# Slot norms moved from the slot matrix to the logits, and combine logits spread between the first expert steps of a soft mixture

## Chip, cores and metric

The kernel runs on one core of one Trainium2 chip. It is one launch that holds a whole twelve-part network (four levels, each of cross attention, attention and feed-forward). The metric is the device time of one execution in microseconds (us).

## The reference, cut to what matters

The change touches two parts of level 1: a linear attention with decay, and after it a soft mixture of 16 experts with 128 slots each, on 2 batches of 128 tokens with 256 features.

```python
# level 1 attention (16 heads of width 16)
q = phi(x @ w_q); k = phi(x @ w_k); v = x @ w_v          # phi(z) = elu(z) + 1
running_kv   = decay_scan(k * v)                          # s_t = decay * s_{t-1} + x_t
running_ksum = decay_scan(k)
den = clip(sum_over_head(q * running_ksum), 1e-6)
x = x + (q * running_kv / den) @ w_out

# level 1 feed-forward: soft mixture, E = 16 experts, S = 128 slots
x_ln = layernorm(x) * gamma + beta
x_n  = x_ln / |x_ln| * scale
mu_n = mu / |mu|                                          # |.| over the 256 features: one number per slot
logits   = einsum('bnd,des->bnes', x_n, mu_n)
dispatch = softmax over tokens n;  combine = softmax over all 2048 slots
slot_in  = einsum('bnd,bnes->besd', x_ln, dispatch)
h        = gelu(slot_in @ W1[e] + b1[e]);  slot_out = h @ W2[e] + b2[e]
x = x + einsum('bsd,bns->bnd', slot_out, combine)
```

## The kernel before, in words

TensorE (PE) multiplies, VectorE (DVE) and ScalarE (ACT) evacuate PSUM and do the elementwise work, GpSimd (POOL) has little to do, SyncE (SP) issues the DMAs. Each of the five runs its own list in order, written out by hand, and they meet at semaphores (`wait_ge`, `then_inc`); `link` makes VectorE wait for its own instruction. Each part of the network is one block, and all engines meet at its end. `k.bank(i)` is one of the eight PSUM banks of 512 float32 columns.

**The slot norms.** The norms of the 2048 slots are found on the way to level 1: `k.mu_norm` holds 1/|mu| in four groups of 32 equal rows, group j for slots 512j to 512j+511 (`l1_xattn`, L1044 and L1084 to L1085).

**`l1_attn`** (L1096 to L1207). PE turns x, makes k, q and v (24 matmul passes with `a_w_qkv`), then with a selecting matrix (`quadrant_rows`) spreads the four groups of `mu_norm` over all partitions in banks 5, 6, 7, 4 (L1139). ACT copies each bank to `row`, which is half of the tensor `mu_squares` (L1162), and POOL multiplies both feature halves of the slot matrix `mu` by it in place, in eight instructions (L1172 to L1177). `mu_ready` counts to 4. Meanwhile DVE makes k and q from the banks (L1187), kv (L1190), and runs the decayed sums as eight scans of 128 elements: four of k into `a_run_k` and four of kv into `a_run_kv` (L1196). It multiplies both by q (L1199, L1200); PE sums over heads (L1142); DVE clips, inverts and multiplies (L1202 to L1204); PE multiplies by `w_out` (L210, from a helper that all accumulating products share); DVE adds to x (L1207).

**`l1_ffn`** (L1214 to L1455). SP issues the loads of b1, W1 (two halves) and W2, all counted by `w_loaded[5]`, and then one small load of b2 for each expert. DVE makes `f_x_ln` and the unit-length `f_x_l`; PE turns the latter (L1263), ACT copies it to `f_x_l_T` (L1349). Then PE computes all combine logits, 128 tokens by 2048 slots for each batch, in eight pieces of 512 columns that fill all eight banks (`combine_logits`); DVE takes the maximum of each piece (L1398), and ACT exponentiates a whole batch at once out of four banks into `comb` (L1352). After that come the experts, as a software pipeline: in step i PE does `dispatch_logits(i)` (4 passes of 256 columns, bank 0), `turn(i-1)` (transposes of two `comb` blocks and of two `disp` blocks, all in bank 1), `gather(i-2)`, `hidden(i-3)`, `slot_out(i-4)` and `combine(i-5)`; the steps run from 0 to 20.

```python
steps = (dispatch_logits, turn, gather, hidden, slot_out, combine)
for i in range(ne + len(steps) - 1):
    for lag, step in enumerate(steps):
        if 0 <= i - lag < ne:
            step(i - lag)
```

`dispatch_logits(i)` may begin once ACT has exponentiated those of i-1 out of the same bank. In step i DVE does `dispatch_max(i)` (L1406, L1408), `take_turned(i-1)` (two copies, `f_disp_tok` and `f_combT`, L1421 and L1424), `take_slots(i-2)` (L1430), `add_bias(i-4)` (L1438) and `dispatch_norm(i)` (L1413, L1415), which waits for ACT's exponentials and lets PE turn them in the next step. ACT does the exponentials of step i (two ACTIVATEs, L1361) and the Gelu of i-3 (L1369). From step 3 on it loads a table before each of the two.

Of the kernel before, what the change touches and what calls it, by code (L numbers as in the profile page):

```python
# [17 lines left out]
P = 128  # L18
# [1077 lines left out]
def l1_attn(k):  # L1096
# [3 lines left out]
    with ExitStack() as ctx:  # L1100
# [8 lines left out]
        row = k.musq[:, 1]  # L1109
# [3 lines left out]
        with signals(nc, k.pool, "dve_step xt_ready proj_ready low_ready exp_ready dec_ready scanned den_in_psum den_ready o_ready out_ready "  # L1113
                     "select_ready row_in_psum row_taken") as s, nc.Block() as block:
# [12 lines left out]
            def _(pe):  # L1127
# [24 lines left out]
            def _(act):  # L1152
# [7 lines left out]
                for j in range(4):  # L1160
                    act.wait_ge(s.row_in_psum, j + 1)
                    nc.scalar.copy(row[:, j * 512:(j + 1) * 512], k.bank(ROW_BANK[j])).then_inc(s.row_taken, 1)  # L1162

            @block.gpsimd
            def _(pool):
# [5 lines left out]
                for j in range(4):  # L1171
                    pool.wait_ge(s.row_taken, j + 1)  # L1172
                    for c in range(DC):
                        sl = slice(j * 512, (j + 1) * 512)
                        last = nc.gpsimd.tensor_tensor(k.mu[:, c, sl], k.mu[:, c, sl], row[:, sl], ALU.mult)
                    last.then_inc(k.mu_ready, 1)

            @block.vector
            def _(dve):
# [5 lines left out]
                for j, bank, dst in ((0, 1, kk), (1, 0, q)):  # L1185
                    dve.wait_ge(s.exp_ready, j + 1)
                    link(nc.vector.scalar_tensor_tensor(out=flat(dst), in0=k.bank(bank), scalar=0.0, in1=ex[:, j],  # L1187
                                                        op0=ALU.max, op1=ALU.add))
                dve.wait_ge(s.proj_ready, 3)
# [24 lines left out]
def l1_ffn(k):  # L1214
# [5 lines left out]
    CR = 6  # L1220
    with ExitStack() as ctx:
        def sb(name, shape, dt=F32):
# [11 lines left out]
        ct = sb("combT", [P, CR, BT])  # L1234
# [6 lines left out]
                 "logits_ready cmax_ready cexp_ready dlog_ready dmax_ready dexp_ready disp_ready "  # L1241
                 "t_in_psum t_taken slot_in_psum slot_taken h_in_psum h_taken so_in_psum so_taken b2_loaded0 b2_loaded1 out_added")
        with signals(nc, k.pool, names) as s, nc.Block() as block:
# [14 lines left out]
            def _(pe):  # L1258

                def turn_x(b):  # L1260
                    pe.wait_ge(s.xs_ready, b + 1)
                    for c in range(DC):
                        last = nc.tensor.transpose(k.bank(7 - b, P, T, c * T), xs[:, b, c * P:(c + 1) * P], k.ident[:])  # L1263
                    last.then_inc(s.xT_in_psum, 1)

                def combine_logits(b, j):
                    pe.wait_ge(s.xT_ready, b + 1)
                    pe.wait_ge(k.mu_ready, j + 1)
                    if b and j >= 2:
                        pe.wait_ge(s.xT_ready, B)  # L1270
                    matmul_acc(nc, k.bank(4 * b + j), [(xst[:, c, b * T:(b + 1) * T], k.mu[:, c, j * 512:(j + 1) * 512]) for c in range(DC)]
                               ).then_inc(s.logits_ready, 1)
                turn_x(0)
                combine_logits(0, 0)
                turn_x(1)
                for j in range(1, 4):
                    combine_logits(0, j)
                for j in range(4):
                    combine_logits(1, j)
                pe.wait_ge(s.cexp_ready, 1)  # L1280

                def dispatch_logits(e):
                    if e >= 1:
# [3 lines left out]
                def turn(e):  # L1287

                    pe.wait_ge(s.cexp_ready, B)
                    if e >= 1:  # L1290
                        pe.wait_ge(s.t_taken, e)
                    for b in range(B):
                        nc.tensor.transpose(k.bank(1, P, P, BT + b * T), comb[:, b, e * SLOTS:(e + 1) * SLOTS], k.ident[:])
# [3 lines left out]
                    last.then_inc(s.t_in_psum, 1)  # L1297

# [27 lines left out]
                def combine(e):  # L1326
                    pe.wait_ge(s.so_taken, B * (e + 1))
                    for b in range(B):
                        last = nc.tensor.matmul(k.bank(5 + b, P, D), ct[:, e % CR, b * T:(b + 1) * T], so[:, e % 2, b],
                                                start=(e == 0), stop=(e == ne - 1))  # L1330
                    last.then_inc(s.out_added, 1)
                steps = (dispatch_logits, turn, gather, hidden, slot_out, combine)
                for i in range(ne + len(steps) - 1):
                    for lag, step in enumerate(steps):
                        if 0 <= i - lag < ne:
                            step(i - lag)

            @block.scalar
            def _(act):
# [7 lines left out]
                for b in range(B):  # L1347
                    act.wait_ge(s.xT_in_psum, b + 1)
                    nc.scalar.copy(xst[:, :, b * T:(b + 1) * T], k.bank(7 - b, P, DC * T).rearrange("p (c t) -> p c t", c=DC)).then_inc(s.xT_ready, 1)  # L1349
                for b in range(B):  # L1350
                    act.wait_ge(s.cmax_ready, b + 1)
                    nc.scalar.activation(comb[:, b], k.ps[:, 4 * b:4 * b + 4].rearrange("p a n -> p (a n)"), ACT.Exp, bias=sm[:, b, 4:5],  # L1352
                                         accum_out=sm[:, b, 5:6]).then_inc(s.cexp_ready, 1)
                act.wait_ge(k.w_loaded[5], 64)
                for i in range(ne + 3):
                    if i < ne:
                        act.wait_ge(s.dmax_ready, B * (i + 1))
# [14 lines left out]
            def _(dve):  # L1372
# [22 lines left out]
                for b in range(B):  # L1395
                    for j in range(4):
                        dve.wait_ge(s.logits_ready, 4 * b + j + 1)
                        last = nc.vector.reduce_max(mx4[:, b, j:j + 1], k.bank(4 * b + j), AX.X)  # L1398
                    link(last)
                    link(nc.vector.reduce_max(sm[:, b, 10:11], mx4[:, b], AX.X))  # L1400
# [1648 lines left out]
```

## Time and profile before

| | |
|---|---|
| median of 3 runs | 1909.32 us (1905.56, 1909.32, 1909.6) |
| the profiled execution | 1906.26 us, its span 1904.5 us |
| PE busy / DVE / ACT / POOL, share of the span | 83% / 61% / 47% / 25% |
| mean granted TensorE clock | 0.911 of full speed |
| `l1_attn` in the trace | 514.4 to about 550.3 us |
| `l1_ffn` in the trace | 550.4 to about 667.6 us |

An engine is busy while an instruction of it runs; a PE that is busy may run at half clock, which the granted clock tells (1.00 is 2.4 GHz, 0.50 is 1.2 GHz). A float32 product appears as two passes, so that a product of 256 features is four matmul records. Averages over the span say nothing on these two blocks, which make up 8% of it, so that everything that follows is read from their own stretch of the trace.

### The profile page before, as it was taken

How to read it: one execution, taken by the hardware profiler on the slowest of the kernel's cores; microseconds unless marked ns; L12 is line 12 of the kernel's file. 1: busy time of each engine (PE TensorE's matmuls, PEld its weight loads, DVE VectorE, ACT ScalarE, POOL GpSimd, SP SyncE). 2: the span in 40 equal slices, each digit the busy share in tenths (PEclk: the TensorE clock that was granted, in tenths of full speed). 3: DMA queues.
4: the chain of work that ended last, by engine and by line, in shares of the span. 5: the costliest groups of instructions: out<-in, count | busy, mean ns of one | idle time of the engine just before them, and what ended most of it. 6: DMA issues, size and time to landing. Idle time of an engine off the chain costs nothing. (4 is left out here: it accounts for less than half of the span.)

```text
span 1904.5 us, 25717 instructions
## 1 busy us (share of the span) xinstructions
PE 1575.8 (83%) x8888; PEld 1102.6 (58%) x8888; DVE 1159.7 (61%) x2417; ACT 886.0 (47%) x1979; POOL 484.8 (25%) x490
## 2 busy tenths in 40 slices
PE   7969888499859988655899999999976578888778
PEld 5644444377536744544577778877752245555567
DVE  5779997366566534545446653455338778888843
ACT  1559988211326532222334533433333478888821
POOL 2350000000020000003322431243000088888810
PEclk9978999699979999657899999999989889999969
DMA  3008999354020000112000000000021322223010
GB/s 122 1 1 161 183 186 178 127 168 146 28 50 14 26 28 1 34 31 98 1 1 1 1 1 1 1 1 1 1 73 55 99 85 82 85 82 100 1 41 32
DMA packets 189501, 110.90 MB, mean 58 GB/s; under 512 B 149129, under 2 KB 165514, under 8 KB 188477
## 3 DMA queue, kind: packets, MB, share of 16 engines
q1 hardware_dynamic: 189372, 109.26, 22.1%
q8 instruction: 73, 1.20, 0.3%
q14 instruction: 56, 0.45, 0.1%
HBM read 75.41 MB, written 0.26 MB: 40 GB/s over the span
## 5 line engine op out<-in xcount | busy, mean ns | idle before, releaser
L210 PE MATMUL banks<-a_w_ring,x_normed_T 128*128 128x512 f32 x320 | 151.1, 613 | 13.2 <-DVEq L2767 5.6
L670 DVE TENSOR_REDUCE x_row_max<-banks 128x1 f32<-128x512 f32 x248 | 152.4, 680 | 15.6 <-PE banks L364 15.5
L573 ACT ACTIVATE x_v_full<-banks,x_neg_max,x_q_scale 128x1024 int16<-128x1024 f32 x128 | 153.2, 1201 | 16.2 <-DMA x_v_full<-x_v_full 8.3
L2721 POOL TENSOR_TENSOR a_t<-a_t,a_bias_ring 128x512 f32<-128x512 f32 x64 | 126.3, 1992 | 129.1 <-DVE a_t L2793 128.9
L2066 PE MATMUL banks<-x_v,x_expsT 128*128 128x128 f32 x1088 | 148.7, 277 | 10.7 <-ACT x_expsT L2224 5.9
L2066 PEld LDWEIGHTS banks<-x_v,x_expsT 128*128 128x128 f32 x1088 | 134.0, 192 | 15.3 <-ACT x_expsT L2224 7.3
L2344 DVE TENSOR_REDUCE x_small<-banks 128x1 f32<-128x2048 f32 x32 | 73.3, 2291 | 86.4 <-PE banks L2047 86.4
L2047 PE MATMUL banks<-x_kT,x_qT 128*128 128x512 f32 x256 | 118.5, 606 | 4.7 <-ACT x_exps L2206 4.7
L2151 POOL TENSOR_TENSOR x_t<-x_t 128x512 f32<-128x512 f32 (+1 forms) x48 | 54.4, 1133 | 260.4 <-DVE x_t L2326 260.4
L364 PE MATMUL banks<-x_kT_parts,x_qT_int 64*128 64x512 bf16 x512 | 104.0, 406 | 6.6 <-DVE x_row_max L670 2.9
L210 PEld LDWEIGHTS banks<-a_w_ring,x_normed_T 128*128 128x128 f32 x320 | 59.9, 195 | 79.8 <-issue 67.8
L425 PEld LDWEIGHTS banks<-x_v_full,x_v_int 128*16 128x16 f16 x1024 | 57.8, 92 | 76.6 <-DMA x_v_full<-x_v_full 47.6
L425 PE MATMUL banks<-x_v_full,x_v_int 128*16 128x128 f16 x1024 | 81.7, 225 | 18.6 <-DMA x_v_full<-x_v_full 18.2
L2354 DVE COPY x_expsT<-banks 128x512 f32<-128x512 f32 (+1 forms) x96 | 53.2, 554 | 71.0 <-PE banks L2055 69.0
L2728 POOL TENSOR_TENSOR a_r<-a_r 128x256 f32<-128x256 f32 x128 | 88.7, 723 | 25.4 <-DVE a_r L2809 25.4
L2055 PE MATMUL banks<-ident,x_exps 128*128 128x128 f32 x544 | 86.3, 274 | 5.4 <-DVE x_expsT L2354 2.6
L2176 ACT ACTIVATE x_squares<-banks 128x512 f32<-128x512 f32 (+1 forms) x48 | 26.1, 544 | 126.6 <-DVE x_t L2326 126.6
L2576 PEld LDWEIGHTS banks<-ident,a_r 128*128 128x128 f32 x256 | 31.8, 150 | 90.4 <-POOL a_r L2728 70.3
L2576 PE MATMUL banks<-ident,a_r 128*128 128x128 f32 x256 | 43.4, 296 | 47.3 <-POOL a_r L2728 47.0
L2047 PEld LDWEIGHTS banks<-x_kT,x_qT 128*128 128x128 f32 x256 | 47.5, 196 | 53.4 <-issue 47.8
L2809 DVE TENSOR_TENSOR a_r<-a_t,ctx_T 128x256 f32<-128x256 f32 x128 | 78.0, 649 | 0.0
L2055 PEld LDWEIGHTS banks<-ident,x_exps 128*128 128x128 f32 x544 | 63.7, 141 | 24.0 <-issue 22.6
(522 smaller groups left out, 3701.5 us busy)
## 6 DMA issues: line engine op xcount, KB each, us to landing
a_w_ring<-in_L_attn_WB_T SPq DMA_DIRECT2D x16, 512.0 KB, 3.7
a_w_ring<-in_L_attn_WC_T SPq DMA_DIRECT2D x16, 512.0 KB, 5.4
f_w_gate_up<-in_L_ffn_gate_up SPq DMA_DIRECT2D x18, 352.0 KB
ctx_tokens<-in_ctx SPq DMA_DIRECT2D x16, 256.0 KB, 5.9
a_w_ring<-in_L_attn_Wth_T SPq DMA_DIRECT2D x8, 512.0 KB, 3.6
a_bias_ring<-in_L_attn_B_bias_perm SPq DMA_DIRECT2D x16, 256.0 KB, 5.0
a_bias_ring<-in_L_attn_C_bias_perm SPq DMA_DIRECT2D x16, 256.0 KB, 6.1
f_w_down<-in_L_ffn_down SPq DMA_DIRECT2D x18, 176.0 KB
```

Of the source, the lines that this page charges most:

```text
L210: last = nc.tensor.matmul(out, lhsT, rhs, start=(i == 0), stop=(i == len(pairs) - 1))
L364: return nc.tensor.matmul(k.bank(bank), qt[lo:lo + 64, h // 2, b * T:(b + 1) * T], kt[lo:lo + 64, h // 2, a:a + 512], start=True, stop=True)
L425: last = nc.tensor.matmul(k.ps[lane:lane + HD, 6, 0:P], vq[:, tile, h * HD:(h + 1) * HD], pt16[:, q % RING, i], start=(tile == 0), stop=(t ...
L573: nc.scalar.activation(eb[:, q % RING], k.ps[:, 2 + 2 * (q % 2):4 + 2 * (q % 2), :].rearrange("p a n -> p (a n)"), ACT.Exp, bias=nb[:, v % ...
L670: nc.vector.reduce_max(mx[:, u % 2, i:i + 1], k.bank(MBANK[m % 3]), AX.X).then_inc(s.max_taken, 1)
L2047: last = nc.tensor.matmul(k.bank(a // 512), qt[:, u % 2, h], kt[:, u % 2, a:a + 512], start=True, stop=True)
L2055: last = nc.tensor.transpose(k.bank(turn_bank(key), P, P, (j % 4) * P), ex[:, n % 2, j * P:(j + 1) * P], k.ident[:])
L2066: last = nc.tensor.matmul(k.bank(7, P, HD3), et[:, (n * NG + g) % 2, j % 4], vt[:, u % 2, j], start=(j == 0), stop=(j == KT3 - 1))
L2576: last = nc.tensor.transpose(k.bank(3, P, P, h * P), r1[:, m % 2, j, h].rearrange("p c n -> p (c n)"), k.ident[:])
L2721: last = nc.gpsimd.tensor_tensor(a, a, bring[:, i % RB, j], ALU.add).then_inc(s.bias_used, 1)
L2728: last = nc.gpsimd.tensor_tensor(a, a, r2[:, j, :, hf], op)
L2809: last = nc.vector.tensor_tensor(r2[:, j, :, hf], t1[:, m % 2, j, :, 1 - hf], ss, ALU.mult)
```

## The change

The slot matrix `mu` is left as it was loaded. The norms go to the logits in two ways:

- **Combine logits** (tokens on partitions, slots in the free dimension): DVE multiplies each piece of 512 by the row of inverse norms, `mu_row`, on its way from PSUM to `comb`, and takes the maximum from there. The row is half of `mu_squares`, which therefore lives on until the end of `l1_ffn`.
- **Dispatch logits** (slots on partitions): the inverse norm is one number per partition, a column of `mu_col`. ACT takes it as the scale of its exponential, DVE as a factor of the negated maximum. `mu_col` is made in `l1_attn` by four transposes of `mu_norm` on PE (into bank 1, once k is out of it) and one ACT copy of 16 columns. POOL's eight multiplications are gone.

The eight pieces of combine logits all go through bank 7, two in each of steps 0 to 3. Transposing `comb` is a step of its own with lag 5 (`turn_combine`, bank 7, one DVE copy `take_combine`), the sum over experts gets lag 6, and the pipeline has 22 steps where it had 21. ACT exponentiates batch 0 of `comb` in step 2 and batch 1 in step 4, in place, between the dispatch exponentials and the Gelu.

```diff
 # l1_attn, PE
+                pe.wait_ge(s.kk_ready, 1)
+                for q4 in range(4):
+                    last = nc.tensor.transpose(k.bank(1, P, P, q4 * P), k.mu_norm[:, q4 * P:(q4 + 1) * P], k.ident[:])
+                last.then_inc(s.col_in_psum, 1)
 # l1_attn, ACT
-                    nc.scalar.copy(row[:, j * 512:(j + 1) * 512], k.bank(ROW_BANK[j])).then_inc(s.row_taken, 1)
+                    nc.scalar.copy(k.mu_row[:, j * 512:(j + 1) * 512], k.bank(ROW_BANK[j])).then_inc(s.row_taken, 1)
+                act.wait_ge(s.col_in_psum, 1)
+                nc.scalar.copy(k.mu_col[:].rearrange("p (j q) -> p q j", j=4), k.bank(1).rearrange("p (q j r) -> p q j r", q=4, j=4)[:, :, :, 0]).then_inc(k.mu_ready, 1)
 # l1_attn, POOL
-                for j in range(4):
-                    pool.wait_ge(s.row_taken, j + 1)
-                    for c in range(DC):
-                        sl = slice(j * 512, (j + 1) * 512)
-                        last = nc.gpsimd.tensor_tensor(k.mu[:, c, sl], k.mu[:, c, sl], row[:, sl], ALU.mult)
-                    last.then_inc(k.mu_ready, 1)
 # l1_ffn, PE
+                def combine_logits(n):
+                    b, j = divmod(n, 4)
+                    pe.wait_ge(s.xT_ready, B)
+                    if n >= 1:
+                        pe.wait_ge(s.logits_taken, n)
+                    matmul_acc(nc, k.bank(7), [(xst[:, c, b * T:(b + 1) * T], k.mu[:, c, j * 512:(j + 1) * 512]) for c in range(DC)]
                                ).then_inc(s.logits_ready, 1)
+                def turn_combine(e):
+                    pe.wait_ge(s.cexp_ready, B)
+                    if e >= 1:
+                        pe.wait_ge(s.ct_taken, e)
+                    for b in range(B):
+                        last = nc.tensor.transpose(k.bank(7, P, P, b * T), comb[:, b, e * SLOTS:(e + 1) * SLOTS], k.ident[:])
+                    last.then_inc(s.ct_in_psum, 1)
...
-                steps = (dispatch_logits, turn, gather, hidden, slot_out, combine)
-                for i in range(ne + len(steps) - 1):
-                    for lag, step in enumerate(steps):
+                steps = ((0, dispatch_logits), (1, turn), (2, gather), (3, hidden), (4, slot_out), (5, turn_combine), (6, combine))
+                for i in range(ne + 6):
+                    for lag, step in steps:
                         if 0 <= i - lag < ne:
                             step(i - lag)
+                        if lag == 0 and i < 4:
+                            combine_logits(2 * i)
+                    if i < 4:
+                        combine_logits(2 * i + 1)
 # l1_ffn, ACT
                 act.wait_ge(k.w_loaded[5], 64)
+                act.wait_ge(k.mu_ready, 1)
                 for i in range(ne + 3):
...
                             nc.scalar.activation(disp[:, i % 2, b * T:(b + 1) * T], k.bank(0, P, T, b * T), ACT.Exp,
-                                                 bias=dm[:, i % 2, b, 1:2], accum_out=dm[:, i % 2, b, 2:3]).then_inc(s.dexp_ready, 1)
+                                                 bias=dm[:, i % 2, b, 1:2], scale=k.mu_col[:, i:i + 1], accum_out=dm[:, i % 2, b, 2:3]).then_inc(s.dexp_ready, 1)
+                    if i in (2, 4):
+                        b = i // 2 - 1
+                        act.wait_ge(s.cmax_ready, b + 1)
+                        nc.scalar.activation(comb[:, b], comb[:, b], ACT.Exp, bias=sm[:, b, 4:5], accum_out=sm[:, b, 5:6]).then_inc(s.cexp_ready, 1)
 # l1_ffn, DVE
+                def take_logits(n):
+                    b, j = divmod(n, 4)
+                    sl = slice(j * 512, (j + 1) * 512)
+                    dve.wait_ge(s.logits_ready, n + 1)
+                    nc.vector.tensor_tensor(comb[:, b, sl], k.bank(7), k.mu_row[:, sl], ALU.mult).then_inc(s.logits_taken, 1)
+                    dve.wait_ge(s.logits_taken, n + 1)
+                    last = nc.vector.reduce_max(mx4[:, b, j:j + 1], comb[:, b, sl], AX.X)
...
-                for i in range(ne + 4):
+                for i in range(ne + 6):
                     if i < ne:
                         dispatch_max(i)
+                    if i < 4:
+                        take_logits(2 * i)
...
-                    if 0 <= i - 4:
+                    if 0 <= i - 4 < ne:
                         add_bias(i - 4)
+                    if 0 <= i - 5 < ne:
+                        take_combine(i - 5)
                     if i < ne:
                         dispatch_norm(i)
+                    if i < 4:
+                        take_logits(2 * i + 1)
```

In the change ACT's wait for `w_loaded[5]` (all expert weights) stands ahead of the first dispatch exponential as it did before, but the combine exponentials no longer come ahead of it.

**PE, start of `l1_ffn`, before** (`f_x_l_T` is xst in the code; L210 with `mu,f_x_l_T` is combine logits, with `f_x_l_T,mu` dispatch logits, with `f_slotT,f_w` the hidden layer):

```order
L1263 MATMUL banks<-ident,f_x_l 128x128 x2
L210 MATMUL banks<-mu,f_x_l_T 128x512 x2
L1263 MATMUL banks<-ident,f_x_l 128x128 x2
L210 MATMUL banks<-mu,f_x_l_T 128x512 x14
L210 MATMUL banks<-f_x_l_T,mu 128x256 x4
L1293 MATMUL banks<-ident,f_combine 128x128 x2
L1296 MATMUL banks<-ident,f_disp 128x128 x2
L210 MATMUL banks<-f_x_l_T,mu 128x256 x2
```

**The same place now:**

```order
L1263 MATMUL banks<-ident,f_x_l 128x128 x4
L210 MATMUL banks<-f_x_l_T,mu 128x256 x2
L210 MATMUL banks<-mu,f_x_l_T 128x512 x4
L210 MATMUL banks<-f_x_l_T,mu 128x256 x2
L210 MATMUL banks<-mu,f_x_l_T 128x512 x2
L1289 MATMUL banks<-ident,f_disp 128x128 x2
L210 MATMUL banks<-mu,f_x_l_T 128x512 x2
L210 MATMUL banks<-f_x_l_T,mu 128x256 x2
L210 MATMUL banks<-mu,f_x_l_T 128x512 x2
L1289 MATMUL banks<-ident,f_disp 128x128 x2
L1308 MATMUL banks<-f_disp_tok,f_x_ln 128x128 x4
```

The sixteen products of the combine logits stood ahead of the first dispatch logits; now they stand in twos behind and between them.

**DVE, one step in the middle of the pipeline, before:**

```order
L1406 TENSOR_REDUCE f_disp_small<-banks 128x2
L1408 TENSOR_SCALAR f_disp_small<-f_disp_small 128x1 x2
L1421 COPY f_disp_tok<-banks 128x256
L1424 COPY f_combT<-banks 128x256
L1430 COPY f_slotT<-banks 128x512
L1438 TENSOR_TENSOR f_slot_out<-banks,f_b 128x256 x2
L1413 RECIPROCAL f_disp_small<-f_disp_small 128x2
L1415 TENSOR_TENSOR f_disp<-f_disp,f_disp_small 128x256
```

**The same step now:**

```order
L1418 TENSOR_REDUCE f_disp_small<-banks 128x2
L1419 TENSOR_SCALAR f_disp_small<-f_disp_small,mu_rnorm_cols 128x2
L1432 COPY f_disp_tok<-banks 128x256
L1444 COPY f_slotT<-banks 128x512
L1452 TENSOR_TENSOR f_slot_out<-banks,f_b 128x256 x2
L1438 COPY f_combT<-banks 128x256
L1424 RECIPROCAL f_disp_small<-f_disp_small 128x2
L1426 TENSOR_TENSOR f_disp<-f_disp,f_disp_small 128x256
```

The copy of the turned combine block has moved from the middle of the step to a place between the bias and the normalisation of the dispatch weights.

## Rows read from the trace of the kernel before

**Rows 1.** Windows: length; busy PE, weight load, DVE, ACT, POOL; granted clock; DMA
```profile
514.50:550.00 35.50, 17.87 (x48) 11.72 (x48) 22.68 (x27) 8.38 (x12) 12.39 (x13) 0.68 0.12 37
...
575.00:663.00 88.00, 84.77 (x432) 63.21 (x432) 51.19 (x155) 53.50 (x107) 0.00 (x0) 0.96 0.09 22
```

**Rows 2.** Groups by line, POOL: busy us, mean ns of one, idle before
```profile
L1175 POOL TENSOR_TENSOR mu<-mu,mu_squares 128x512 f32<-128x512 f32 x8 | 11.1, 1425 | 12.5 <-ACT mu_squares L1162 12.5
```

**Rows 3.** Timeline of the attention, DVE and POOL: start us, us, instruction
```profile
528.11 3.42 DVE L1196 TENSOR_TENSOR_SCAN a_run_k<-a_decay,a_k 128x128 f32<-128x128 f32 x4
528.45 11.14 POOL L1175 TENSOR_TENSOR mu<-mu,mu_squares 128x512 f32<-128x512 f32 x8 [12.53 <-ACT mu_squares L1162]
531.45 5.42 DVE L1196 TENSOR_TENSOR_SCAN a_run_kv<-a_decay,a_kv 128x128 f32<-128x128 f32 x4
536.90 1.57 DVE L1199 TENSOR_TENSOR a_run_k<-a_run_k,a_q 128x512 f32<-128x512 f32 x1
...
540.71 0.69 DVE L1202 TENSOR_SCALAR a_k<-banks 128x512 f32<-128x512 f32 x1 [0.57 <-PE banks L1142]
544.82 0.69 DVE L1204 TENSOR_TENSOR a_run_kv<-a_run_kv,a_kv 128x512 f32<-128x512 f32 x1
```

**Rows 4.** The same timeline from 529.0 on: the third scan alone
```profile
528.76 1.43 DVE L1196 TENSOR_TENSOR_SCAN a_run_k<-a_decay,a_k 128x128 f32<-128x128 f32 x1
```

**Rows 5.** Timeline of the attention, PE
```profile
526.72 3.60 PE L1139 MATMUL banks<-mu_norm,quadrant_rows 128*128 128x512 f32 x8
538.52 2.08 PE L1142 MATMUL banks<-a_run_k,head_blocks 128*128 128x256 f32 x4 [8.21 <-DVE a_run_k L1199]
545.66 3.75 PE L210 MATMUL banks<-a_w_out,a_run_kv 128*128 128x256 f32 x8 [5.06 <-DVE a_run_kv L1204]
```

**Rows 6.** Windows of 1 us in which the granted clock changes
```profile
533.00:534.00 1.00, 0.00 (x0) 0.00 (x0) 1.00 (x1) 0.00 (x0) 1.00 (x2) 0.96 0.00 0
561.00:562.00 1.00, 1.00 (x3) 0.43 (x2) 0.00 (x0) 1.00 (x1) 0.00 (x0) 0.89 1.13 185
...
585.00:586.00 1.00, 1.00 (x9) 0.90 (x8) 0.84 (x3) 0.00 (x0) 0.00 (x0) 0.94 0.00 0
```

**Rows 7.** Timeline of the mixture, PE: start of the logits, first steps, steps 6 and 7
```profile
556.27 3.78 PE L210 MATMUL banks<-mu,f_x_l_T 128*128 128x512 f32 x4 [0.46 <-ACT f_x_l_T L1349]
...
560.27 12.65 PE L210 MATMUL banks<-mu,f_x_l_T 128*128 128x512 f32 x28
...
576.88 1.13 PE L210 MATMUL banks<-f_x_l_T,mu 128*128 128x256 f32 x4 [3.09 <-ACT f_disp L1361]
...
579.61 2.08 PE L210 MATMUL banks<-f_x_l_T,mu 128*128 128x256 f32 x4 [1.14 <-ACT f_disp L1361]
...
598.07 1.03 PE L210 MATMUL banks<-f_x_l_T,mu 128*128 128x256 f32 x4
...
603.39 1.03 PE L210 MATMUL banks<-f_x_l_T,mu 128*128 128x256 f32 x4
```

**Rows 8.** The load of W2: SP's issue in the timeline, and its time to landing
```profile
553.05 2.14 SPq L1249 DMA_DIRECT2D f_w<-in_L_ffn_W  x1
...
f_w<-in_L_ffn_W SPq DMA_DIRECT2D x1, 1024.0 KB, 11.0
```

**Rows 9.** Timeline of step 7, DVE and ACT
```profile
603.39 0.43 DVE L1415 TENSOR_TENSOR f_disp<-f_disp,f_disp_small 128x256 f32<-128x256 f32 x1
...
605.16 0.37 ACT L1361 ACTIVATE f_disp<-banks,f_disp_small 128x128 f32<-128x128 f32 x1 [1.43 <-DVE f_disp_small L1408]
```

**Rows 10.** The unit-length x of the two batches: ns min/median/max, first and last start
```profile
L1394 DVE TENSOR_SCALAR f_x_l<-f_x_ln,f_small,x_scale x2: 412/412/413, 554.6 to 555.6; 128x256 f32<-128x256 f32 x2
```

**Rows 11.** The exponential of a batch of combine logits: ns min/median/max, first and last start
```profile
L1352 ACT ACTIVATE f_combine<-banks,f_small x2: 1967/1967/1967, 567.2 to 574.1; 128x2048 f32<-128x2048 f32 x2
```

**Rows 12.** Timeline of the end of the mixture
```profile
664.34 2.05 PE L1329 MATMUL banks<-f_slot_out,f_combT 128*128 128x256 f32 x8
...
666.49 0.88 DVE L1454 SCALAR_TENSOR_TENSOR x_res<-banks,f_small,x_res 128x256 f32<-128x256 f32 x2 [1.03 <-PE banks L1329]
```

More of the change, by code:

```diff
@@ L1113, in l1_attn @@
         with signals(nc, k.pool, "dve_step xt_ready proj_ready low_ready exp_ready dec_ready scanned den_in_psum den_ready o_ready out_ready "
-                     "select_ready row_in_psum row_taken") as s, nc.Block() as block:
+                     "select_ready row_in_psum row_taken col_in_psum kk_ready") as s, nc.Block() as block:
             @block.sync
@@ L1188, in _ @@
                                                         op0=ALU.max, op1=ALU.add))
+                    if j == 0:
+                        dve.sem_inc(s.kk_ready, 1)
                 dve.wait_ge(s.proj_ready, 3)
@@ L1219, in l1_ffn @@
     ns = ne * SLOTS
-    CR = 6
     with ExitStack() as ctx:
@@ L1262, in turn_x @@
                     for c in range(DC):
-                        last = nc.tensor.transpose(k.bank(7 - b, P, T, c * T), xs[:, b, c * P:(c + 1) * P], k.ident[:])
+                        last = nc.tensor.transpose(k.bank(5 + b, P, T, c * T), xs[:, b, c * P:(c + 1) * P], k.ident[:])
                     last.then_inc(s.xT_in_psum, 1)
[L1266 to L1271, printed above, removed]
+                def combine_logits(n):
[4 more added lines that the diff above has]
+                    matmul_acc(nc, k.bank(7), [(xst[:, c, b * T:(b + 1) * T], k.mu[:, c, j * 512:(j + 1) * 512]) for c in range(DC)]
                                ).then_inc(s.logits_ready, 1)
                 turn_x(0)
-                combine_logits(0, 0)
                 turn_x(1)
[L1276 to L1280, printed above, removed]
                 def dispatch_logits(e):
-                    if e >= 1:
+                    if e == 0:
+                        pe.wait_ge(s.xT_ready, B)
+                    else:
                         pe.wait_ge(s.dexp_ready, B * e)
@@ L1287, in turn @@
                 def turn(e):
-                    pe.wait_ge(s.cexp_ready, B)
                     if e >= 1:
                         pe.wait_ge(s.t_taken, e)
-                    for b in range(B):
-                        nc.tensor.transpose(k.bank(1, P, P, BT + b * T), comb[:, b, e * SLOTS:(e + 1) * SLOTS], k.ident[:])
                     pe.wait_ge(s.disp_ready, e + 1)
@@ L1348, in _ @@
                     act.wait_ge(s.xT_in_psum, b + 1)
[L1349 to L1353, printed above, removed]
+                    nc.scalar.copy(xst[:, :, b * T:(b + 1) * T], k.bank(5 + b, P, DC * T).rearrange("p (c t) -> p c t", c=DC)).then_inc(s.xT_ready, 1)
                 act.wait_ge(k.w_loaded[5], 64)
+                act.wait_ge(k.mu_ready, 1)
                 for i in range(ne + 3):
                     if i < ne:
-                        act.wait_ge(s.dmax_ready, B * (i + 1))
+                        act.wait_ge(s.dmax_ready, i + 1)
                         if i >= 2:
@@ L1394, in _ @@
                     nc.vector.tensor_scalar(xs[:, b], xl[:, b], sm[:, b, 9:10], k.xscale[:, 0:1], ALU.mult, ALU.mult).then_inc(s.xs_ready, 1)
[L1395 to L1400, printed above, removed]
-                    nc.vector.tensor_scalar(sm[:, b, 4:5], sm[:, b, 10:11], -1.0, None, ALU.mult).then_inc(s.cmax_ready, 1)
+                def take_logits(n):
[5 more added lines that the diff above has]
+                    last = nc.vector.reduce_max(mx4[:, b, j:j + 1], comb[:, b, sl], AX.X)
+                    if j == 3:
+                        link(last)
+                        link(nc.vector.reduce_max(sm[:, b, 10:11], mx4[:, b], AX.X))
+                        nc.vector.tensor_scalar(sm[:, b, 4:5], sm[:, b, 10:11], -1.0, None, ALU.mult).then_inc(s.cmax_ready, 1)
                 def dispatch_max(e):
@@ L1406, in dispatch_max @@
                     link(nc.vector.tensor_reduce(dm[:, r, :, 0], k.bank(0, P, BT).rearrange("p (b t) -> p b t", b=B), AX.X, ALU.max))
-                    for b in range(B):
-                        nc.vector.tensor_scalar(dm[:, r, b, 1:2], dm[:, r, b, 0:1], -1.0, None, ALU.mult).then_inc(s.dmax_ready, 1)
+                    nc.vector.tensor_scalar(dm[:, r, :, 1], dm[:, r, :, 0], k.mu_col[:, e:e + 1], -1.0, ALU.mult, ALU.mult).then_inc(s.dmax_ready, 1)
                 def dispatch_norm(e):
@@ L1420, in take_turned, with take_combine @@
                         dve.wait_ge(s.slot_in_psum, e - 1)
-                    link(nc.vector.tensor_copy(dtk[:, e % 2], k.bank(1, P, BT)))
-                    if e >= CR:
-                        dve.wait_ge(s.out_added, e - CR + 1)
-                    nc.vector.tensor_copy(ct[:, e % CR], k.bank(1, P, BT, BT)).then_inc(s.t_taken, 1)
+                    nc.vector.tensor_copy(dtk[:, e % 2], k.bank(1, P, BT)).then_inc(s.t_taken, 1)
+                def take_combine(e):
+                    dve.wait_ge(s.ct_in_psum, e + 1)
+                    if e >= 2:
+                        dve.wait_ge(s.out_added, e - 1)
+                    nc.vector.tensor_copy(ct[:, e % 2], k.bank(7, P, BT)).then_inc(s.ct_taken, 1)
                 def take_slots(e):
```

13 lines of the change are left out of this document (8 added, 5 removed).

## Prediction

> **What bounds the kernel now.** The chain of waits that the profile follows back reaches only into the last part of the network, so I read the two changed blocks from their own stretch: windows first, then the timeline engine by engine, then what ended each idle time.
>
> In the attention no engine is full, and VectorE is the busiest [rows 1]. POOL's only work there is the rescaling of the slot matrix, eight products of 1.4 us [rows 2], and the timeline shows what it does to its neighbour. POOL starts at 528.45. The first two scans start before that, 0.33 us apart (528.11, and the third at 528.76 [rows 3, 4]); the third takes 1.43 us, and the four kv scans take 5.42 us together, 1.35 each. The product behind them takes 1.57 us, where the same shape takes 0.69 once POOL is done [rows 3]. PE waits 8.21 us for that product [rows 5]. So the block is bound by VectorE, and VectorE by POOL.
>
> In the mixture PE is busy for 84.8 of the 88 us of the steps, at 0.96 of its clock [rows 1]: PE bounds it, at 5.32 us a step once the pipeline is full (603.39 - 598.07 [rows 7]). What is not PE's own work lies at the start: the logits begin at half clock, which lasts to about 561.2 [rows 6]; then PE stands idle for 3.09 and 1.14 us, waiting for the first dispatch exponentials [rows 7], and after that it runs at half clock again from 579.6 (2.08 us for what took 1.13 [rows 7]) to about 585.1 [rows 6].
>
> **The change, part by part, attention.** Without POOL the eight scans take 8 x 0.33 = 2.6 us from 528.11, to 530.8; the product takes 0.69, to 531.5, where PE began the sums over heads at 538.52 [rows 3, 5]: 7.0 us less. PE is free by then: its spreading of the norms ends at 530.3 [rows 5] and the four added transposes (passes of 128 columns, 0.11 each, a quarter of the 12.65/28 = 0.45 for a pass of 512 [rows 7]) end at 530.8. Since it has hardly been idle, it does the sums at full clock, 1.13 instead of 2.08 us [rows 5, 7]: 1.0 us less. The rest of the chain (L1202 to the addition) keeps its lengths. The output product too: PE will have been idle for some 5 us before it, and before the change the clock fell at about 534.0, after 3.7 idle us [rows 5, 6], so I leave its 3.75 us at half clock. The added ACT copy of 16 columns lies beside the scans; if it didn't, it would cost a few tenths. The increment that VectorE issues for PE costs under 0.1. **Attention: -8.0 us.** Bounds: 0, if the scans are slow by themselves from the third on; -9.9, if the output product comes at full clock.
>
> **The change, mixture, start to step 7.** I count PE's time between the logits' start and the dispatch logits of step 7 (556.27 to 603.39 [rows 7]).
> - The first product now needs both batches of x turned. VectorE finishes the second 0.9 us behind the first [rows 10]: +0.9.
> - Work that leaves this stretch: the second turning of x (0.4, now ahead of it), five pairs of turned combine blocks (0.22 each, two passes of 128) and one combine (1.0, half of 2.05 [rows 12]). -2.5. All but the first 0.4 comes back at the end.
> - The second half-clock stretch goes, 5.5 us at half: -2.7. This supposes that PE is kept busy enough.
> - The two idle times go, 3.09 + 1.14 [rows 7], and some 0.3 in step 5: -4.5.
> - New waits take their place. Each piece uses bank 7 and waits until VectorE has multiplied the last: 0.1 to notice, 0.69 for 512 columns, out of PSUM and for a product alike (L1202, L1204 [rows 3]), 0.05 back. Step 0: the second piece follows the first directly, 0.9. Step 1: ACT's first exponential waits for W2, which lands at 553.05 + 11.0 = 564.05 [rows 8]; the exponentials end at 564.9. PE's two pieces, the first at half clock, end then too, so PE itself loses nothing, but VectorE's normalisation and then its second product come behind the exponentials, at 566.2, and PE, through with its dispatch logits at 565.8, waits 0.4. The fourth piece waits 0.7 (only the 0.22 of `turn` lies between). Steps 2 and 3: gather and hidden lie between, 0.4 in all. Step 2 also has ACT's exponential of batch 0, 2.0 us [rows 11] plus 0.2 to read the sum, which the 5.8 us of PE's step cover.
> - Step 4: the last product and maximum of VectorE stand ahead of `dispatch_max(4)`, and the exponential of batch 1 (2.2) stands between ACT's dispatch exponentials and its two table loads and Gelu. ACT's slack in a full step is 1.43 us [rows 9]. What is left over comes out in step 5: 0.75 before `turn(4)`, 0.5 before `hidden(2)`. Step 6, which still runs behind, 0.85: `take_combine` stands ahead of the normalisation for which PE waits. With 0.4 of small gaps the new waits make +4.9.
>
> Together 0.9 - 2.5 - 2.7 - 4.5 + 4.9 = -3.9.
>
> **Full steps.** The same work on PE. On VectorE the combine copy (0.42) moves to right ahead of the normalisation. That ended 0.43 us into PE's step [rows 9]; now 0.43 + 0.45 - 0.22 (the bias can start earlier, since a pair of transposes has moved behind `slot_out`) = 0.66, and PE needs it at 0.87, behind the dispatch logits. Slack 0.2 us: no cost. It is thin; each 0.1 us over it would cost 1 us in ten steps. ACT has its 1.43 us.
>
> **Last steps.** The 2.1 us of moved transposes and the moved combine fall due: +2.1. In step 16 no dispatch logits cover the 0.66: about +0.4 against before. The last combine comes after another copy and a combine, but these are the moved work, counted already; noticing costs 0.1. In all +2.5 less 0.2 that the old end already waited. **Mixture: -3.9 + 2.3 = -1.6 us.** Bounds: +3, if every new wait is half as long again; -5, if half of them is hidden.
>
> The first exponential now takes its scale from a column instead of none, 32 ACTIVATEs in all. No row here has such a form; its nearest, the same ACTIVATE with a bias alone, is covered by the 1.43 us in full steps [rows 9]. I take 0, between 0 and the 1.43.
>
> The Trainium skill (ScalarE: Activation LUTs, What ACT_TABLE_LOAD costs) states that each pointer operand adds about 93 ns to an ACTIVATE; that speaks against the change. No run here shows it yet. By it 0.19 us would be added in each of the four early steps in which the exponentials are waited for, an estimate from that page of 0.8 us, and the sum would be -8.8 rather than -9.6.
>
> **Sum.** -8.0 - 1.6 = -9.6 us. Against the profiled execution, 1906.26: 1896.7. The median of the runs is 1909.32, 3.1 above it, which gives 1899.7. Between the two I say **1898.0**, which is 1907.6 less 9.6. The block ends earlier as a whole and nothing behind it depends on anything else, so that nothing gives the gain back.
>
> **Rivals**, each against 1907.6.
> - *The mixture gives nothing.* The new waits in the first steps are as long as the old idle times and the longer end costs its 2.3. For it: seven waits that were not there, all through one bank. Against: PE has two pieces to do where it had nothing. Gain 5 to 8, about 1901.
> - *More than forecast.* The output product at full clock (-1.9) and half of the new waits hidden (-2.5): 1893.6. For it: the idle time before that product is only a little over the 3.7 us after which the clock fell.
> - *The attention gives nothing*, the scans being slow by themselves. Then only -1.6, 1906. Against it: the plain product of two SBUF operands shows the same, 1.57 against 0.69 [rows 3], and all slow instructions lie within POOL's 11.1 us.
> - *Slower: PE stays at half clock through the first steps.* The new waits cut its work into short pieces from 562 to 599. That stretch holds some 30 us of PE's work, which would take 30 more, of which the waits of 4.9 absorb that much: +25 - 9.6 = +15, 1923. It decides from about 20 us more at half clock. Against it: the old trace fell to half clock behind 3.09 and 1.14 us of idle close together [rows 6, 7], and no new wait is over 0.9. The Trainium skill (TensorE: Matmul & The Clock Gate, A second HAM failure mode) describes just this, short idle times between groups that make the clock fall back again and again; in this trace a busy share of 0.96 held the full clock [rows 1].
>
> **How the numbers follow.** A measurement of this kernel can tell 0.2%, 3.8 us, from no change. Forecast 0.60, nothing from the mixture 0.20, more 0.12, nothing from the attention 0.04, slower 0.04. The range 1890.5 to 1903.5 holds the first two whole and most of the third, with some 2 us either way for which execution the median is. Faster by over 0.2%: 0.60 + 0.20 + 0.12 = 0.92. Within: 0.04. Slower: 0.04.
>
> **What would show it.** Eight scans within 2.7 us; the product behind them at 0.69; the sums over heads at full clock, 7 to 8 us after the first scan less than before; first dispatch exponential right at the landing of W2; no half clock between 562 and the end of the mixture; full steps of 5.32 us; the mixture 1 to 3 us shorter. Wrong: scans still over 1 us without POOL, full steps over 5.4, or a second stretch at half clock.

## The result

| | before | changed |
|---|---|---|
| median | 1909.13 us (19 runs, 1904.5 to 1914.0) | 1914.41 us (19 runs, 1910.23 to 1923.6) |
| profiled execution | 1906.26 | 1917.02 |
| ratio | | 1.0032, 95% interval 1.0021 to 1.0044 |

The change made the kernel slower by 0.32%, where 0.5% faster was forecast. The attention did what it should. All of the loss and more lies in the mixture, and there behind step 6. In the traces below the two blocks together are 8.9 us longer, and the profiled executions differ by 10.8; the medians differ by 5.3. The profiled execution of the changed kernel lies 2.6 us above its median and that of the kernel before 2.9 us below, so that the traces overstate the loss. In which part a median execution is shorter than these traces is not known.

**The profile after.** First the timeline of VectorE in the attention of the changed kernel (start, length, instruction), which answers to [rows 3, 4]:

```profile
529.55 1.37 DVE L1197 TENSOR_TENSOR_SCAN a_run_k<-a_decay,a_k 128x128 f32<-128x128 f32 x4
530.84 1.35 DVE L1197 TENSOR_TENSOR_SCAN a_run_kv<-a_decay,a_kv 128x128 f32<-128x128 f32 x4
532.22 0.69 DVE L1200 TENSOR_TENSOR a_run_k<-a_run_k,a_q 128x512 f32<-128x512 f32 x1
...
534.21 0.69 DVE L1203 TENSOR_SCALAR a_k<-banks 128x512 f32<-128x512 f32 x1 [0.69 <-PE banks L1145]
```

Eight scans take 2.67 us instead of 8.8, and the product 0.69 instead of 1.57. PE in the same stretch, against [rows 5]:

```profile
531.62 0.60 PE L1141 MATMUL banks<-ident,mu_norm 128*128 128x128 f32 x4
532.97 1.13 PE L1145 MATMUL banks<-a_run_k,head_blocks 128*128 128x256 f32 x4 [0.74 <-DVE a_run_k L1200]
539.16 3.75 PE L210 MATMUL banks<-a_w_out,a_run_kv 128*128 128x256 f32 x8 [5.06 <-DVE a_run_kv L1205]
```

The sums over heads run at full clock, the output product still at half. From SP's first load of the attention to its first load of the mixture passed 35.96 us before and 28.49 now: -7.5.

The mixture, measured the same way to the first load of the next block, took 117.24 us before and 133.61 now. Split at dispatch logits 7 and 15:

| us | before | changed | forecast for the difference |
|---|---|---|---|
| block start to dispatch logits 7 | 53.00 | 49.43 | -3.9 |
| dispatch logits 7 to 15, eight full steps | 42.56 | 52.07 | 0 |
| dispatch logits 15 to the end | 21.68 | 32.11 | +2.3 |

The early steps gained 3.6 us. Every full step lost 1.19 us, and the end lost 10.4 instead of 2.3. Windows of the changed kernel over the attention and these three stretches (length; busy PE, weight load, DVE, ACT, POOL; granted clock; DMA share, GB/s):

```profile
515.40:543.90 28.50, 17.66 (x52) 12.03 (x52) 14.78 (x27) 8.54 (x14) 1.31 (x5) 0.76 0.15 46
543.90:593.30 49.40, 40.71 (x152) 23.41 (x153) 30.36 (x78) 26.97 (x55) 0.00 (x0) 0.90 0.29 54
593.30:645.40 52.10, 43.77 (x226) 31.12 (x225) 26.08 (x72) 33.05 (x57) 0.00 (x0) 1.00 0.08 21
645.40:677.50 32.10, 25.48 (x109) 16.90 (x107) 12.54 (x34) 4.26 (x10) 0.00 (x0) 0.89 0.06 17
```

In the full steps PE is busy for 43.8 of 52.1 us at full clock, where it was nearly always busy [rows 1]. No engine is full any more, so it is a wait. One full step of the changed kernel in the timeline:

```profile
598.96 1.03 PE L1332 MATMUL banks<-f_slot_out,f_combT 128*128 128x256 f32 x4
...
599.82 1.03 PE L210 MATMUL banks<-f_x_l_T,mu 128*128 128x256 f32 x4
600.12 0.76 DVE L1452 TENSOR_TENSOR f_slot_out<-banks,f_b 128x256 f32<-128x256 f32 x2 [2.71 <-PE banks L1332]
600.79 0.41 DVE L1438 COPY f_combT<-banks 128x256 f32<-128x256 f32 x1
...
601.12 0.16 DVE L1424 RECIPROCAL f_disp_small<-f_disp_small 128x2 f32<-128x2 f32 x1
601.32 0.42 DVE L1426 TENSOR_TENSOR f_disp<-f_disp,f_disp_small 128x256 f32<-128x256 f32 x1
...
601.89 0.41 PE L1289 MATMUL banks<-ident,f_disp 128*128 128x128 f32 x2 [1.04 <-DVE f_disp L1426]
...
602.38 0.46 ACT L1365 ACTIVATE f_disp<-banks,f_disp_small,mu_rnorm_cols 128x128 f32<-128x128 f32 x1 [2.43 <-DVE f_disp_small L1419]
```

Read backwards: PE stands idle for 1.04 us before the transposes; it waits for the normalisation (L1426); that is queued behind the copy (L1438) and the bias (L1452); and the bias, whose input from `slot_out` has long been there, was released by L1332, PE's **combine**, after VectorE had stood idle for 2.71 us. The list of waits over the mixture says the same for all steps: who waits, for whom, us in total, times, longest. Before the change:

```profile
DVE f_slot_out L1438 <- PE banks L1323: 22.5, 16, 2.4
```

and after it:

```profile
DVE f_slot_out L1452 <- PE banks L1332: 39.8, 14, 5.5
...
PE banks L1289 <- DVE f_disp L1426: 12.3, 12, 1.9
```

The bias now waits 14 of 16 times for the combine and not for its own input (L1323). The reason is in two lines that the diff does not touch. `slot_out` has two buffers, and the bias of expert e overwrites that of e-2, for which it waits until the combine of e-2 is done. With lag 5 this combine ran in the step before (`add_bias(i-4)`, combine of i-6 in step i-1). With lag 6 it runs in the same step, and last in it. So each step became a loop: combine, bias, copy, normalisation, transposes, four more pieces of PE's work (gather, hidden layer, slot outputs, the turned combine blocks), combine. The change also cut the ring of turned combine blocks (`f_combT`) from six buffers to two. That ring is not what holds the steps up: run 1 below keeps it at two.

### The profile page after: what moved, and what is told of

It is laid out like the page before. It is cut to its first block and busy times, and to the rows that moved or that the text cites. A ratio compares the mean times of both kernels' runs of the same rounds, so it can differ in the third digit from the quotient of the medians.

```text
span 1915.2 us, 25750 instructions
## 1 busy us (share of the span) xinstructions
PE 1577.1 (82%) x8892; PEld 1101.4 (58%) x8892; DVE 1155.7 (60%) x2409; ACT 889.2 (46%) x1980; POOL 475.4 (25%) x482
## 5 line engine op out<-in xcount | busy, mean ns | idle before, releaser
L210 PE MATMUL banks<-a_w_ring,x_normed_T 128*128 128x512 f32 x320 | 151.3, 614 | 13.2 <-DVEq L2788 5.6
L573 ACT ACTIVATE x_v_full<-banks,x_neg_max,x_q_scale 128x1024 int16<-128x1024 f32 x128 | 153.3, 1202 | 15.2 <-DMA x_v_full<-x_v_full 10.5
L2087 PE MATMUL banks<-x_v,x_expsT 128*128 128x128 f32 x1088 | 148.7, 277 | 10.8 <-ACT x_expsT L2245 5.9
L210 PEld LDWEIGHTS banks<-a_w_ring,x_normed_T 128*128 128x128 f32 x320 | 60.2, 196 | 79.8 <-issue 67.8
```

The source lines that it names most:

```text
L210: last = nc.tensor.matmul(out, lhsT, rhs, start=(i == 0), stop=(i == len(pairs) - 1))
L573: nc.scalar.activation(eb[:, q % RING], k.ps[:, 2 + 2 * (q % 2):4 + 2 * (q % 2), :].rearrange("p a n -> p (a n)"), ACT.Exp, bias=nb[:, v % ...
L2087: last = nc.tensor.matmul(k.bank(7, P, HD3), et[:, (n * NG + g) % 2, j % 4], vt[:, u % 2, j], start=(j == 0), stop=(j == KT3 - 1))
```

## The experiments

**1. Three slot-output buffers.** The changed kernel with one more buffer:

```diff
-        ht, so = sb("hT", [HID, 2, BT]), sb("slot_out", [P, 2, B, D])
+        ht, so = sb("hT", [HID, 2, BT]), sb("slot_out", [P, 3, B, D])
...
-                    if e >= 2:
-                        dve.wait_ge(s.out_added, e - 1)
+                    if e >= 3:
+                        dve.wait_ge(s.out_added, e - 2)
                     for b in range(B):
-                        nc.vector.tensor_tensor(so[:, e % 2, b], k.bank(4, P, D, b * D), b2[:, e % 2], ALU.add).then_inc(s.so_taken, 1)
+                        nc.vector.tensor_tensor(so[:, e % 3, b], k.bank(4, P, D, b * D), b2[:, e % 2], ALU.add).then_inc(s.so_taken, 1)
```

(and `so[:, e % 3, b]` in `combine`.)

> The changed kernel with three buffers for the biased slot outputs instead of two, and the bias of expert e waiting for the combine of e-3 instead of e-2. Theory A (the lag of 6 with two buffers puts the combine of the same step ahead of the bias): the bias no longer waits for L1332, full steps fall from 6.51 to 5.3 to 5.4 us, the mixture from 133.6 to 116 to 119 us, the time to about 1899, faster than before. Rival B (the combine copy that now stands ahead of the normalisation eats VectorE's slack, as the prediction feared): full steps stay at 6.0 us or more, time 1908 or more. Rival C (splitting the transposes costs PE itself): steps stay at 6.5, time unchanged.

Measured: 1896.73 us (6 runs) against 1907.28, ratio 0.9945 (0.9932 to 0.9959). Full steps 5.27 us, the mixture 114.99. Its timeline in a full step:

```profile
608.36 0.76 DVE L1452 TENSOR_TENSOR f_slot_out<-banks,f_b 128x256 f32<-128x256 f32 x2 [1.38 <-PE banks L1325]
608.53 1.03 PE L1332 MATMUL banks<-f_slot_out,f_combT 128*128 128x256 f32 x4
...
609.03 0.42 DVE L1438 COPY f_combT<-banks 128x256 f32<-128x256 f32 x1
...
609.56 0.42 DVE L1426 TENSOR_TENSOR f_disp<-f_disp,f_disp_small 128x256 f32<-128x256 f32 x1
610.25 0.38 PE L1289 MATMUL banks<-ident,f_disp 128*128 128x128 f32 x2
...
611.18 0.46 ACT L1365 ACTIVATE f_disp<-banks,f_disp_small,mu_rnorm_cols 128x128 f32<-128x128 f32 x1 [1.20 <-DVE f_disp_small L1419]
```

The bias waits for its input again (L1325) and runs beside the combine. PE has no idle time before the transposes: the normalisation ends at 609.98, 0.27 us before they start. Theory A holds. B and C fall: the copy still stands ahead of the normalisation and the transposes are still split, and steps are slightly shorter than before the change (5.27 against 5.32 us). The mixture came out below the 116 to 119 us that were expected.

**2. The kernel before with the lag alone.**

```diff
-                for i in range(ne + len(steps) - 1):
-                    for lag, step in enumerate(steps):
+                for i in range(ne + len(steps)):
+                    for lag, step in zip((0, 1, 2, 3, 4, 6), steps):
```

> The kernel before with one part of the change alone: combine at lag 6 instead of 5, everything else as it was (norms on the slot matrix, logits up front, transposes together, two slot-output buffers). Theory A: the bias waits for the combine of its own step; then 0.3 us to notice, 0.67 for the bias, 0.6 for the normalisation, 0.05 back stand against 1.09 of PE's work, so full steps grow from 5.32 to about 5.9 us, the time by 6 to 9 us to about 1916. Rivals B and C: neither the copy nor the transposes have moved, so full steps stay at 5.32 and the time grows by under 2 us (one more step).

Measured: 1915.38 us (6 runs), ratio 1.0036 (1.0023 to 1.0049): this one number costs the old kernel as much time as the whole change did, which also has 7.5 us of gain in the attention to set against its loss. Full steps 5.94 us, the mixture 125.76, and in the timeline:

```profile
616.00 0.76 DVE L1438 TENSOR_TENSOR f_slot_out<-banks,f_b 128x256 f32<-128x256 f32 x2 [2.53 <-PE banks L1329]
...
617.35 0.44 PE L1296 MATMUL banks<-ident,f_disp 128*128 128x128 f32 x2 [0.40 <-DVE f_disp L1415]
```

**3. The attention's part alone.** The kernel before without POOL's products (the slots stay without their norms):

```diff
-                    for c in range(DC):
-                        sl = slice(j * 512, (j + 1) * 512)
-                        last = nc.gpsimd.tensor_tensor(k.mu[:, c, sl], k.mu[:, c, sl], row[:, sl], ALU.mult)
-                    last.then_inc(k.mu_ready, 1)
+                    pool.sem_inc(k.mu_ready, 1)
```

> The kernel before with POOL's eight multiplications of the slot matrix left out (the slots are then not normalised; nothing else changes). It prices the attention's part alone. Theory: scans 2.7 us instead of 8.8, the attention 7.5 to 8 us shorter, the mixture as before (117 us), and the time 7.5 to 8 us under before, about 1901: the gain of the attention is real and not given back behind it. Rival: the gain is taken back behind it by the granted clock, time within 3 us of before.

Measured: 1898.71 us (5 runs), ratio 0.9955 (0.9942 to 0.9968), 8.6 us less. The attention took 28.52 us, 7.4 less than before, and the mixture 116.65. Nothing of the gain is given back. The scans:

```profile
527.77 1.37 DVE L1193 TENSOR_TENSOR_SCAN a_run_k<-a_decay,a_k 128x128 f32<-128x128 f32 x4
529.05 1.35 DVE L1193 TENSOR_TENSOR_SCAN a_run_kv<-a_decay,a_kv 128x128 f32<-128x128 f32 x4
```

**4. The combine copy behind the normalisation**, still with two buffers:

```diff
-                    if 0 <= i - 5 < ne:
-                        take_combine(i - 5)
                     if i < ne:
                         dispatch_norm(i)
+                    if 0 <= i - 5 < ne:
+                        take_combine(i - 5)
```

> The changed kernel with the combine copy behind the normalisation on VectorE, still two slot-output buffers. Theory A: the copy (0.42) leaves the chain from combine to bias to normalisation to transposes, but the chain stays: full steps 6.51 - 0.42 = 6.1 us. Rival B: full steps come back to 5.3 to 5.4 us, since the copy alone made the normalisation late. Rival C: 6.5.

Measured: full steps 6.17 us (6.51 in the changed kernel), time 1908.21 (a single execution). The bias still waits for the combine:

```profile
609.56 0.76 DVE L1452 TENSOR_TENSOR f_slot_out<-banks,f_b 128x256 f32<-128x256 f32 x2 [2.71 <-PE banks L1332]
...
610.99 0.41 PE L1289 MATMUL banks<-ident,f_disp 128*128 128x128 f32 x2 [0.71 <-DVE f_disp L1426]
```

So of the 1.19 us a step the copy's place was worth 0.34, and only while the loop stood: with three buffers (run 1) the same place costs nothing. The other 0.85 belongs to the loop that the lag and two buffers make. Run 2 has 0.62 of it. The 0.23 that is left is about what the pair of turned combine blocks takes (0.27 from their start to that of the combine, 608.12 to 608.39 in run 4's trace): in run 2 PE does them while it waits for the normalisation, and in the changed kernel they stand between the slot outputs and the combine, inside the loop. This last share is worked out from the rows; no run changes it alone.

**5 to 7. What is left in the early steps.** All three start from run 1. Run 5 moves ACT's wait for the expert weights:

```diff
-                act.wait_ge(k.w_loaded[5], 64)
                 act.wait_ge(k.mu_ready, 1)
...
+                    if e == 0:
+                        act.wait_ge(k.w_loaded[5], 64)
                     act.wait_ge(s.h_in_psum, e + 1)
```

> e1 (three slot-output buffers) with ACT's wait for the expert weights moved from the first dispatch exponential to the first Gelu. In e1 the first exponential stands 2.29 us waiting for W2, but PE has two pieces of combine logits to do meanwhile. Theory: it costs little, since what follows on PE also waits for the second piece: the dispatch logits of step 7 start 0.3 to 1.0 us earlier than the 48.99 us of e1 after the block's start. Rival: the load sets the pace of the early steps, and 2.3 us or more come off.

Run 6 gives the combine logits two banks:

```diff
-                    if n >= 1:
-                        pe.wait_ge(s.logits_taken, n)
-                    matmul_acc(nc, k.bank(7), [(xst[:, c, b * T:(b + 1) * T], k.mu[:, c, j * 512:(j + 1) * 512]) for c in range(DC)]
+                    if n >= 2:
+                        pe.wait_ge(s.logits_taken, n - 1)
+                    matmul_acc(nc, k.bank(7 - n % 2), [(xst[:, c, b * T:(b + 1) * T], k.mu[:, c, j * 512:(j + 1) * 512]) for c in range(DC)]
```

> e1 with the pieces of combine logits alternating between banks 7 and 6, so that a piece waits for VectorE's take of the one before the last. Theory: the waits of 0.87, 0.16 and 0.66 us ahead of pieces two to four go, with some tenths later, and the dispatch logits of step 7 start 1.5 to 2.5 us earlier than in e1. Rival: VectorE's two passes over each piece (1.4 us of the 1.9 of PE) are the bound behind the bank, and under 0.5 us comes off.

Run 7 has both, and the copy behind the normalisation:

> e1 with both edits of e5 and e6 and the combine copy behind the normalisation. Expected: the sum of the two, the 0.57 us ahead of the transposes of step 5 also gone, full steps still at 5.27; 2 to 4 us under e1, about 1893 to 1895, and the ratio to before about 0.993. Rival: the early steps have another bound behind these waits (ACT with the exponential of a whole batch between its table loads), and the time stays within 1 us of e1.

Measured, from the traces (time: a single execution for 5 and 6, the median of 6 runs for 1 and 7):

| us | start to dispatch logits 7 | full step | to the end | mixture | time |
|---|---|---|---|---|---|
| 1, three buffers | 48.99 | 5.27 | 23.81 | 114.99 | 1896.73 |
| 5, weights at the Gelu | 48.76 | 5.27 | 23.82 | 114.76 | 1906.77 |
| 6, two logit banks | 47.03 | 5.27 | 23.81 | 113.03 | 1894.98 |
| 7, all together | 45.90 | 5.27 | 23.48 | 111.57 | 1893.37 |

The wait for W2 was worth 0.23 us by itself, just under the 0.3 to 1.0 expected: the second piece of logits holds PE anyway. The single bank was worth 1.96, as expected. Together they gave 3.09, more than the sum of 2.19: 0.33 of it in step 6, from the copy's place, and most of the rest in step 0 (7.04 us, and 7.74 with the banks alone). Without the bank's wait PE is through with its two pieces earlier, and the load is what it waits for: in run 6 it stands idle for 0.49 us ahead of the dispatch logits of step 1, until the exponentials that waited for W2 are done. PE at the start of the mixture in the changed kernel, with the waits that the single bank made:

```profile
552.54 3.62 PE L210 MATMUL banks<-mu,f_x_l_T 128*128 128x512 f32 x4
557.03 1.96 PE L210 MATMUL banks<-mu,f_x_l_T 128*128 128x512 f32 x4 [0.88 <-DVE f_combine L1407]
558.94 1.13 PE L210 MATMUL banks<-f_x_l_T,mu 128*128 128x256 f32 x4
560.30 1.96 PE L210 MATMUL banks<-mu,f_x_l_T 128*128 128x512 f32 x4 [0.22 <-DVE f_combine L1407]
562.09 0.38 PE L1289 MATMUL banks<-ident,f_disp 128*128 128x128 f32 x2
563.13 1.95 PE L210 MATMUL banks<-mu,f_x_l_T 128*128 128x512 f32 x4 [0.66 <-DVE f_combine L1407]
```

and in run 7:

```profile
551.22 5.34 PE L210 MATMUL banks<-mu,f_x_l_T 128*128 128x512 f32 x8
556.40 1.03 PE L210 MATMUL banks<-f_x_l_T,mu 128*128 128x256 f32 x4
557.26 1.88 PE L210 MATMUL banks<-mu,f_x_l_T 128*128 128x512 f32 x4
558.98 0.38 PE L1289 MATMUL banks<-ident,f_disp 128*128 128x128 f32 x2
559.20 1.88 PE L210 MATMUL banks<-mu,f_x_l_T 128*128 128x512 f32 x4
```

Run 7 beats both kernels: 1893.37 us (1888.37 to 1894.89) against 1908.53, ratio 0.9913 (0.9895 to 0.993). The single times of runs 4, 5 and 6 say little of their edits (11 runs of the kernel before beside runs 5 to 7 spread from 1903.95 to 1913.43), and run 5's nothing: its trace is 10 us longer than run 1's behind the mixture (1246.4 against 1236.1 us), in blocks that it doesn't touch.

## Why the prediction was wrong

**The step that failed is "Full steps. The same work on PE", with its "no cost".** It followed the copy, the bias and the normalisation on VectorE and ACT's slack, and did not ask what the bias itself waits for. It read the new lag as one more step at the end; it is also a longer life for each slot output, and two buffers no longer covered it. The term that failed is the end of the normalisation: the sum let the bias start 0.22 us earlier and put that end 0.66 us into PE's step. In the changed kernel it came 1.92 us into the step (601.74, the step beginning at 599.82), where PE needed it at 0.87; with the third buffer it came at 0.59 (609.98, from 609.39). So the slack that the text counted holds (0.2 us forecast and 0.27 measured behind the normalisation; 1.43 forecast and 1.20 measured on ACT), but only in a kernel without the missed wait. The measured price is 1.19 us a step, 9.5 us over eight steps.

**The end** was forecast at +2.3 and came at +10.4. Its steps waited in the same way, and in one stretch (655.4 to 662.2) PE ran at half clock besides, behind 1.90 us of idle time ahead of the transposes. That stretch is worth some 3.4 us, half its length (an estimate). In run 4, which has the loop too, the end ran at full clock throughout and took 28.19 us. With three buffers, also at full clock, it was 23.81 - 21.68 = +2.1.

**The rest of the sum held**, which run 1 shows, being the forecast's kernel without the missed wait:
- Attention: forecast -8.0, measured -7.5. From the first scan to the end of the block it was 14.34 us instead of 22.28, the -8.0 of the forecast: the scans, the product and the sums over heads came as worked out. The 0.5 that is missing lies ahead of them: the products for q, k and v took 8.15 us and not 7.60, the full clock having come 10.3 us after the block's start instead of 9.3. The output product stayed at half clock, as taken. Run 3 shows that nothing of the gain is given back.
- Start to step 7: forecast -3.9, measured -3.6, and -4.0 in run 1. The waits at the single bank were put at 0.9, 0.4 and 0.7 and came at 0.88, 0.22 and 0.66; those of steps 5 and 6 were put at 0.75, 0.5 and 0.85 and came at 0.41, 0.54 and 0.57. Against that, PE ran at half clock for 5.75 us from its first product instead of 4.95. So a part of the agreement is errors that cancel. The second half-clock stretch did not come: the granted clock is 1.00 from 556.4 on, 0.90 over the whole start. W2 landed at 557.9 (11.2 us after its issue at 546.72), and the first dispatch exponential started at 557.90, as forecast.
- Mixture with the buffer: 114.99 against 117.24, -2.3 where -1.6 was forecast (the start -4.0, eight full steps -0.4, the end +2.1). Time: 1907.28 x 0.9945, that is -10.5 where -9.6 was forecast.

**The rivals.** The one that ended slower, PE at half clock through the first steps, did not happen; the slowdown came from a mechanism that none of them named. The 0.2 us of slack behind the normalisation, which the text called thin, were enough: 0.27 in run 1. "Full steps over 5.4" stood among the signs that would show the forecast wrong, and it is the sign that did.

**The price of the scale column.** The row for the new form in the changed kernel, in the full step above (602.38), is 0.46 us; without the scale it was 0.37 [rows 9]. The medians of the 32 are 0.453 and 0.363, 0.09 more for each. The forecast took 0; it lies beside PE's work in full steps (ACT stood idle for 1.20 us ahead of it in run 1 even so), and in the early steps the measured start still came within 0.3 of the sum.

The Trainium skill (ScalarE: Activation LUTs, What ACT_TABLE_LOAD costs) gives about 93 ns for a pointer operand; this trace agrees. Whether it made the early steps longer by the 0.8 us estimated from that figure can't be told from the other terms here.

## What to carry to other kernels

In a software pipeline over a ring of buffers, a lag is a buffer lifetime: before moving a consumer by a step, list every producer that waits for it to free a buffer, and where in the step that consumer now stands. If producer and freeing consumer fall in the same step with the consumer last, the step becomes a serial loop, and where that loop is longer than the busiest engine's work (here 5.94 and 6.51 us against 5.3) it sets the pace, whatever slack each engine shows. And read the releaser of each wait as well as its length: the bias waited before the change too (22.5 us in 16 waits), but for its input.

## What the runs showed of the hardware

VectorE's scans of 128 elements, both operands in SBUF, took 0.40 us alone and 1.41 beside POOL's products of two SBUF operands (1.37 each), so that one VectorE instruction went with each POOL instruction; eight scans in a row without POOL took 2.67 us. The product of 512 with both operands in SBUF took 0.69 and 1.57. The rows of before show the scans beside POOL [rows 3, 4]; run 3 and the changed kernel show all eight without it.

The Trainium skill (SBUF — State Buffer, Who interferes with whom) states that a VectorE instruction with two SBUF inputs contends with a GpSimd instruction that reads SBUF, and calls the ports that the two share an exclusive lock. These rows agree on the contention, for the scans too. That one waits for the whole of the other fits the one-to-one pace, but no row shows POOL's product without VectorE beside it, so that it is not shown here.

When the full clock comes in a block changed from trace to trace by more than a microsecond, without any change in the block: in the attention, with the same instructions, it came 10.4, 8.8, 9.2 and 8.7 us after the block's start in runs 1, 5, 6 and 7, and the block took 28.51, 27.83, 27.69 and 27.33 us. Each is one trace, so that these don't tell the kernel from the execution. A term of under a microsecond in such a block can't be read from one trace.
